# Splitting the rounding of context and tiles between ScalarE and VectorE, with reordered expert stage, in a decoder block

## The reference

```
x = x + attention(layernorm(x))           # 32 query heads, 8 key/value heads of 128, rope, causal
x = x + matmul(fake_quant(layernorm(x)), fake_quant(ctx))   # ctx 2 x 1024 x 1024
x = x + experts(layernorm(x))             # 64 experts of rank 8, the top 16 of 64 by a router, softmax gate
fake_quant(x): q = clip(round(x / s + z), 0, 255); return (q - z) * s
```

## Time and profile before

| what | value |
|---|---|
| time, median of 3 runs | 1343.87 us (1343.54 to 1347.83) |
| the profiled execution's own time | 1344.35 us |
| its span, first to last instruction | 1342.6 us |
| mean granted TensorE clock | 0.987 of full |
| TensorE busy | 1273.5 us, 95% |
| VectorE, ScalarE, GpSimd busy | 831.3, 772.8, 613.9 us |

### The profile page before, as it was taken

One profiled execution on the slowest core, in us unless ns is written; L12 is line 12 of the kernel. 1 busy time (PEld: TensorE's weight loads), 2 busy tenths in 40 slices (PEclk: granted clock), 3 DMA queues, 4 the chain that ended last, 5 costly groups with the idle time before them and its releaser, 6 DMA issues. The chain is left out here.

```text
span 1342.6 us, 19909 instructions
## 1 busy us (share of the span) xinstructions
PE 1273.5 (95%) x7016; PEld 1095.6 (82%) x7025; DVE 831.3 (62%) x1805; ACT 772.8 (58%) x1587; POOL 613.9 (46%) x454
## 2 busy tenths in 40 slices
PE   5899999999999999999999979899999998988998
PEld 4779998888888888888888868778888887667777
DVE  7797135555556555565555555456877769787753
ACT  3512237667777777777777768753333454654530
POOL 5677666678758677777776745310000000201100
PEclk9999999999999999999999989899999999989999
DMA  7033144548659468485673976888653485000001
GB/s 266 9 134 126 48 153 162 156 130 217 210 159 251 143 179 243 122 215 139 160 207 111 236 214 199 234 239 260 218 157 126 162 279 166 23 1 16 32 32 47
DMA packets 117122, 207.42 MB, mean 154 GB/s; under 512 B 10128, under 2 KB 51088, under 8 KB 113440
## 3 DMA queue, kind: packets, MB, share of 16 engines
q1 hardware_dynamic: 112992, 176.79, 39.9%
q0 software_dynamic: 4032, 29.36, 11.8%
HBM read 147.40 MB, written 88.08 MB: 175 GB/s over the span
## 5 line engine op out<-in xcount | busy, mean ns | idle before, releaser
L1225 DVE TENSOR_TENSOR pT_lo<-banks,pT_hi 128x512 fp32r<-128x512 f32 (+1 forms) x192 | 103.7, 596 | 184.9 <-ACT pT_hi L963 184.9
L1609 PE MATMUL banks<-ob_hi,oa_hi 128*128 128x512 f32 x384 | 149.7, 390 | 4.5 <-DVE ob_lo L1257 3.8
L1609 PE MATMUL banks<-ob_hi,oa_lo 128*128 128x512 f32 x384 | 149.4, 389 | 0.0
L1609 PE MATMUL banks<-ob_lo,oa_hi 128*128 128x512 f32 x384 | 149.4, 389 | 0.0
L1804 POOL TENSOR_TENSOR resid<-resid,colterm 128x1024 f32<-128x1024 f32 x8 | 19.8, 2490 | 274.4 <-ACT colterm L1861 184.4
L1567 PE MATMUL banks<-xc,nring_hi_a 128*128 128x512 f32 x448 | 140.0, 394 | 1.3 <-DVE q_made L1175 1.3
L1567 PE MATMUL banks<-xc,nring_hi_b 128*128 128x512 f32 x448 | 139.8, 393 | 0.0
L947 ACT CAST oa_hi<-oraw 128x1024 fp32r<-128x1024 f32 x48 | 50.4, 1050 | 146.9 <-PE banks L1609 142.7
L963 ACT CAST pT_hi<-banks 128x512 fp32r<-128x512 f32 (+1 forms) x192 | 86.5, 525 | 76.6 <-PE banks L1537 76.4
L1234 DVE CUSTOM_DVE_ANT_0 prob<-banks,mask 128x512 f32<-128x512 f32 (+3 forms) x256 | 109.8, 485 | 0.3 <-DVE resid L1153 0.3
L728 POOL TENSOR_TENSOR q_lo<-q_raw,q_hi 128x512 fp32r<-128x512 f32 x64 | 87.0, 1360 | 40.5 <-ACT q_hi L901 40.4
(11 more groups left out here) (245 smaller groups left out, 3483.2 us busy)
## 6 DMA issues: line engine op xcount, KB each, us to landing
q_raw<-qk_dram SPq DMA_DIRECT2D x64, 256.0 KB, 3.9
o_S<-o_st SPq DMA_DIRECT2D x64, 256.0 KB, 3.9
w<-in_L_attn_Wo SPq DMA_DIRECT2D x32, 512.0 KB, 6.5
oraw<-o_S SPq DMA_DIRECT2D x32, 512.0 KB, 3.7
nraw<-in_L_attn_Wq SPq DMA_DIRECT2D x28, 512.0 KB, 5.7
o_S<-o_S POOLq DMA_DIRECT2D x12, 1024.0 KB, 10.7
o_S<-o_N POOLq DMA_DIRECT2D x12, 1024.0 KB, 9.7
resid<-in_x SPq DMA_DIRECT2D x16, 512.0 KB, 6.4
```

What stands on the lines that cost most here:

```text
L1225: nc.vector.tensor_tensor(pT[1][:, sl], turned_chunk(turned, mixed, c), as32(pT[0][:, sl]), ALU.subtract).then_inc(pT_lo, 1)
L1609: ins = nc.tensor.matmul(step_bank(m, t), oa[a][:, s % 2, k, t * P:(t + 1) * P], ob[c][:, s % 2, k, :], start=(q == 0 and k == 0 and i == ...
```

## The change

It does the following. (a) At the start GpSimd makes w_low(3) ahead of the weight sums, and the sums wait until VectorE has normalised its four tiles. (b) `load_first(0)` and `load_first(1)` move ahead of the stores of turned heads, with weaker waits. (c) The copy of banks 6 and 7 after step 7 moves from ScalarE to VectorE. (d) The ctx rounding is split: ScalarE scales and clamps at 0 (Relu), VectorE takes the minimum with 255 and adds MAGIC, ScalarE takes off the constant (unmagic) into bf16. (e) The additions of p1 after product P5 are spread over four steps. (f) Tiles of x are rounded in the same three parts. (g) In the expert loop the transposes of the next tile (`x` fills) move ahead of turn_quantised and expand, and the parts of each tile are put in another order on ScalarE and VectorE.

In the order's rows, raw is the buffer of a tile being rounded, q its quantised bf16 form, norm and xe the normalised tile and its transposed parts, part the read-out product, zT the gated transposed values.

The diff, shortened (declarations, arguments and lines that only follow the same move are left out):

```diff
@@ -541,7 +542,8 @@
             if f == 0:
                 for n in (26, 27):
                     sp.wait_ge(o_kept[n % 2], o_count(n))
-                sp.wait_ge(job_read, 6 * NARROW)
+            if f < 2:
+                sp.wait_ge(job_read, 6 * NARROW - 1 + f)
             if f >= 2:
                 sp.wait_ge(fa_lo, f - 1)
             q, half = f % PAIRS, f // PAIRS
@@ -613,6 +615,8 @@
+            if u == LAST_JOB_UNIT + 1:
+                load_first(0)
...
+            if u == LAST_JOB_UNIT + 1:
+                load_first(1)
-                load_first(f)
+                if f >= 2:
+                    load_first(f)
...
@@ -797,10 +805,11 @@
         w_low(0)
         w_low(1)
         w_low(2)
+        w_low(3)
+        pool.wait_ge(ln_out_v, TPB)
         weight_sum(0, "S1")
         weight_sum(0, "S3")
         weight_sum(0, "S2")
-        w_low(3)
         for n in range(2 * TPB):
             turn_sum(n)
         w_low(4)
...
@@ -924,18 +933,19 @@
+            if f == 1:
+                act.wait_ge(q_kept[0], 64 * NARROW)
-        def keep_first(f):
-            if f % PAIRS == PAIRS - 1:
-                act.wait_ge(first_done, f + 1)
-                for n in range(2):
-                    nc.scalar.copy(p1[:, 2 * (f // PAIRS) + n, :], banks[:, 6 + n, :]).then_inc(first_read, 1)
+        def keep_second_pass():
+            act.wait_ge(first_done, FIRST_STEPS)
+            for n in range(2):
+                nc.scalar.copy(p1[:, 2 + n, :], banks[:, 6 + n, :]).then_inc(first_read, 1)
...
 
         def scale_ctx(n):
             act.wait_ge(ctx_in[n % 2], 16 * (n // 2 + 1))
-            nc.scalar.activation(raw[:, n % 2, :], raw[:, n % 2, :], ACT.Identity, bias=Z2, scale=R2
+            nc.scalar.activation(raw[:, n % 2, :], raw[:, n % 2, :], ACT.Relu, bias=Z2, scale=R2
                                  ).then_inc(c_scaled, 1)
+
+        def quant_ctx(n):
+            act.wait_ge(c_rounded, n + 1)
+            if n == 0:
+                act.wait_ge(one_made, 1)
+            nc.scalar.activation(q2[:, n, :], raw[:, n % 2, :], ACT.Identity, bias=unmagic[:, 0:1], scale=1.0
+                                 ).then_inc(c_quant, 1)
 
         root(0)
         ln_scale(1)
...
@@ -1060,17 +1073,20 @@
-        keep_first(FIRST_STEPS - 1)
+        keep_second_pass()
+            if 1 <= n:
+                quant_ctx(n - 1)
+        quant_ctx(2 * KT - 1)
-            nc.scalar.activation(raw[:, t, :], resid[:, t, :], ACT.Identity, bias=scl[:, 1, t:t + 1],
+            nc.scalar.activation(raw[:, t, :], resid[:, t, :], ACT.Relu, bias=scl[:, 1, t:t + 1],
...
             nc.vector.tensor_tensor(ob[1][:, f % 2, :, :], w00[:, 2 * q:2 * q + 2, :], as32(ob[0][:, f % 2, :, :]),
                                     ALU.subtract).then_inc(fb_lo, 1)
 
+        def keep_first_pass():
+            dve.wait_ge(first_done, PAIRS)
+            for n in range(2):
+                nc.vector.tensor_copy(p1[:, n, :], banks[:, 6 + n, :]).then_inc(first_read, 1)
+
...
@@ -1311,17 +1330,17 @@
-                elif p == "P5":
-                    link(nc.vector.tensor_tensor(rows(1, 1, tp), p1_pair(tp), rows(1, 1, tp), ALU.add))
-                    link(nc.vector.tensor_tensor(rows(1, 0, tp), p1_pair(tp), rows(1, 0, tp), ALU.add))
-
-        def quant_ctx(n):
+
+        def add_copy(tp, half):
+            dve.wait_ge(out_read, 2 * OUT.index("P7") + 2)
+            for t in (2 * tp, 2 * tp + 1):
+                dve.wait_ge(x_in[TPB + t], 32)
+            link(nc.vector.tensor_tensor(rows(1, half, tp), p1_pair(tp), rows(1, half, tp), ALU.add))
+
+        def round_ctx(n):
-            nc.vector.tensor_scalar(raw[:, n % 2, :], raw[:, n % 2, :], MAGIC, MAGIC, ALU.add, ALU.max
+            nc.vector.tensor_scalar(raw[:, n % 2, :], raw[:, n % 2, :], 255.0, MAGIC, ALU.min, ALU.add
-            dve.wait_ge(c_rounded, n + 1)
-            nc.vector.tensor_scalar(q2[:, n, :], raw[:, n % 2, :], MAGIC + 255.0, MAGIC + MIDDLE,
-                                    ALU.min, ALU.subtract).then_inc(c_quant, 1)
...
@@ -1413,6 +1432,8 @@
+            if (u, 1) in STEP_AT and STEP_AT[u, 1] == PAIRS - 1:
+                keep_first_pass()
@@ -1423,11 +1444,13 @@
-                quant_ctx(s - 4 * PAIRS)
+                round_ctx(s - 4 * PAIRS)
+            if m == 4 and 3 <= q < 7:
+                add_copy((q - 3) // 2, (q - 3) % 2)
...
@@ -1760,6 +1784,8 @@
+        if i + 1 < TT:
+            lb_order += [("x", 2 * i + 2), ("x", 2 * i + 3)]
...
@@ -1814,8 +1840,16 @@
-            nc.scalar.activation(v1[:, t % 2, :], resid[:, t, :], ACT.Identity, bias=scl[:, 1, t:t + 1],
+            nc.scalar.activation(v1[:, t % 2, :], resid[:, t, :], ACT.Relu, bias=scl[:, 1, t:t + 1],
+
+        def quantise(t):
+
+            act.wait_ge(v_rounded, t + 1)
+            if t >= 2:
+                act.wait_ge(q_turned, t - 1)
+            nc.scalar.activation(q1[:, t % 2, :], v1[:, t % 2, :], ACT.Identity, bias=unmagic[:, 0:1], scale=1.0
+                                 ).then_inc(v_quant, 1)
...
@@ -1900,23 +1938,26 @@
         root(2)
         copy_turned(3)
         exponentials(0)
-        late_root(TPB)
+        highs("x", (2, 3))
+        normalise(2)
         for i in range(1, TT):
-            highs("x", (2 * i, 2 * i + 1))
-            if i + 1 < TT:
-                normalise(i + 1)
-            if i + 3 < TT:
-                scale_tile(i + 3)
             if i + AHEAD < TT:
                 read_product(i + AHEAD)
             high("z", i - 1)
+            if i == 1:
+                highs("b", range(6, 8))
+            if i + 3 < TT:
+                late_root(i + 3)
+                scale_tile(i + 3)
             if i + AHEAD < TT:
                 root(i + AHEAD)
-            if i == 1:
-                highs("b", range(6, 8))
+            if i + 3 < TT:
+                quantise(i + 3)
             exponentials(i)
-            if i + 4 < TT:
-                late_root(i + 4)
+            if i + 1 < TT:
+                highs("x", (2 * i + 2, 2 * i + 3))
+            if i + 2 < TT:
+                normalise(i + 2)
             if i + 3 < TT:
                 copy_turned(i + 3)
         high("z", TT - 1)
...
@@ -1938,15 +1979,12 @@
-        def quantise(t):
+        def round_tile(t):
-            link(nc.vector.tensor_scalar(v1[:, t % 2, :], v1[:, t % 2, :], MAGIC, MAGIC, ALU.add, ALU.max))
-            if t >= 2:
-                dve.wait_ge(q_turned, t - 1)
-            nc.vector.tensor_scalar(q1[:, t % 2, :], v1[:, t % 2, :], MAGIC + 255.0, MAGIC + MIDDLE,
-                                    ALU.min, ALU.subtract).then_inc(v_quant, 1)
+            nc.vector.tensor_scalar(v1[:, t % 2, :], v1[:, t % 2, :], 255.0, MAGIC, ALU.min, ALU.add
+                                    ).then_inc(v_rounded, 1)
...
@@ -2033,31 +2074,37 @@
+        product_stats(1)
-        quantise(3)
+        round_tile(3)
+        product_stats(2)
+        lows("x", (2, 3))
-            lows("x", (2 * i, 2 * i + 1))
+            if i + AHEAD < TT:
+                row_term(i + AHEAD)
+                add_product(i + AHEAD)
+            low("z", i - 1)
+            if i == 1:
+                lows("b", range(6, 8))
+            if i + AHEAD < TT:
+                product_stats(i + AHEAD)
-                row_term(i + AHEAD)
-                add_product(i + AHEAD)
+                scale_of(i + AHEAD)
-                quantise(i + 3)
-            low("z", i - 1)
-            if i + AHEAD < TT:
-                scale_of(i + AHEAD)
-            if i == 1:
-                lows("b", range(6, 8))
+                round_tile(i + 3)
+            if i + 1 < TT:
+                lows("x", (2 * i + 2, 2 * i + 3))
...
@@ -2200,6 +2247,8 @@
+            if i + 1 < TT:
+                turn_fills("x", (2 * i + 2, 2 * i + 3))

```

More of the change, by code:

```diff
@@ L127, in build @@
         one = sb("one", [P, P], BF16)
+        unmagic = sb("unmagic", [P, 1], F32)
         banks = whole.enter_context(nc.psum_tensor("banks", [P, 8, 512], F32))
@@ L190, in build @@
             b_rows = sb4("b_rows", [P, D // P, NR], F32)
-            shared = (resid, ident, identb, stats, moments, rstd, lnw, mean_rstd, scal, calc, scl, one, raw,
+            shared = (resid, ident, identb, stats, moments, rstd, lnw, mean_rstd, scal, calc, scl, one, unmagic, raw,
                       a_rows, b_rows, q2, banks, KT, TT, TPB, H)
@@ L251, in attention @@
               A_w, B_w, proj, heads, narrow, outp, resid, ident, identb, stats, moments, rstd, lnw, mean_rstd, scal,
-              calc, scl, one, raw, a_rows, b_rows, q2, banks, KT, TT, TPB, H):
+              calc, scl, one, unmagic, raw, a_rows, b_rows, q2, banks, KT, TT, TPB, H):
     _, sem = held
@@ L677, in _ @@
         nc.gpsimd.tensor_copy(identb[:], ident[:]).then_inc(ident_made, 1)
+        nc.gpsimd.memset(unmagic[:], -(MAGIC + MIDDLE)).then_inc(one_made, 1)
         nc.gpsimd.memset(one[:], 1.0).then_inc(one_made, 1)
@@ L1036, in _ @@
```

(27 more changed lines are left out.)

## The result

The changed kernel takes 1356.98 us (median of 6 runs, 1352.64 to 1360.64) against 1344.62 (6 runs, 1343.54 to 1347.83) for the kernel before: ratio 1.0075, 95% interval 1.0058 to 1.0092, so 0.75% slower. (Every ratio here is the recorded estimate from all runs; the two medians divided give 1.0092, and elsewhere too they differ from the ratio by up to 0.0017.) Predicted was 1351.0, in the range 1339.5 to 1358. The profiled execution took 1352.64, the shortest of the six; its span is 1350.9 at a mean clock of 0.982.

What follows compares the result with a forecast made beforehand. TensorE, busy 95% of the time, was taken as the bound, other engines costing only where it waits. Terms −2.0, −6.5, −4.4, +2.3 and +17.6 sum to +7.0 on 1344.35, 1351.4, put at 1351.0 for the median; range 1339.5 to 1358.

Steps and rivals of the forecast that it cites:

- Start: At the start, VectorE's row-scale multiplications no longer held beside GpSimd's sums, so the fill begins earlier: −2.0 us.
- First step: First step of the output projection: earlier load of oraw removes a 4.6 us wait and the low clock behind it, −6.5.
- Step 8: Output projection, step 8: moving the copy to VectorE removes TensorE's 3.8 us wait and the half clock behind it, −4.4.
- fourth rival: First 900 us: waits move on to VectorE and half of 12.9 is lost, about 1357 us; chance 0.05.
- ctx: Ctx stage: loads no longer overlap, cycle 6.1 against 5.44 us, lag +6.1, less a 3.8 wait; net +2.3.
- third rival: Ctx stage: the reload of ctx is slower than its median, +7 instead of +2.3, 1355.7 us; chance 0.1.
- Expert loop: Expert stage: GpSimd's addition holds scale_of, TensorE waits 4.7, a tile costs +3.4; with the clock the stage costs +17.6.
- second rival: Expert loop: VectorE's scale_of gets past GpSimd's addition, TensorE idles 2.3, about 1339 us, faster; chance 0.2.
- the first four turns go this way: Expert loop, i = 1 to 4: each turn costs +3.4 over an old 19.06 us, 13.6 in all.
- stand behind other work of TensorE for the most part; I count 0 to 3 and take 0: Prologue of the expert stage: ScalarE's new instructions delay first products 0, 2 and 3; 0 to 3 us, taken as 0.
- The clock: Expert stage: idles of 4.7 us lower TensorE's clock, 1.7 × 3 = 5.1, and 1.1 at the first turn.
- first rival: Expert stage: idles of 4.7 don't lower the clock, stage costs 11.4, total 1344.7 us, no change; chance 0.2.

Runs made afterwards that it cites:

- e1_front: The change in attention() alone, with the expert stage of the kernel before; ratio 0.9952 to the kernel before.
- e2_expert: The change in mix_and_experts() alone, with attention() of the kernel before; ratio 1.0129 to the kernel before.
- e7_front_swap: e1_front with ScalarE taking off the constant of ctx tile n - 1 ahead of scaling tile n; 1334.35 us, ratio 0.9904 to the kernel before.
- e3_pool_late: The changed kernel with GpSimd's addition to tiles 4 to 7 waiting for VectorE's rounding instead of ScalarE's scaling; ratio 0.9992 to the kernel before.
- e6_warm_full: The changed kernel with 76 further TensorE transposes (120 for tile 4) ahead of turn_quantised of tiles 4 to 7; ratio 1.0041 to the kernel before.
- e4_warm: The changed kernel with 40 further TensorE transposes ahead of each turn_quantised of tiles 4 to 7; ratio 1.0067 to the kernel before.
- e9_stats_later: e7_front_swap with VectorE's product statistics moved behind the tile's rounding and zT_lo in the expert stage; ratio 0.9901 to the kernel before.

## Why the prediction was right, and where only its sum was

The forecast of 1351.0 is 6.0 short of the measured median and inside the range. The front was forecast at −10.6 and is −6.5 in e1_front's time; the expert stage was forecast at +17.6 and is +17.4 in e2_expert's, for reasons that were only partly the forecast ones. Term by term:

- **Start, −2.0.** Measured 3.6 alone (2.2 to 5.1). The wait of 4.21 fell to 1.00 and one of 2.83 on xc came, as the prediction's "t3 gives the rest back" has it; the two traces are 1.7 apart at 57 us and 1.3 at 790, which explains less than half of the 3.6.
- **First step, −6.5.** Right: 6.2 alone (3.6 to 8.6). In the trace of the changed kernel it shows as 5.6, since the half clock behind the wait before it (3.3 long in both traces, ending at 789.39 and at 790.65) lasted 1.0 longer there.
- **Step 8, −4.4.** The mechanism as put ("stood behind high parts that waited for a transfer") is right, but "ahead of nothing that waits for a transfer" is not enough: VectorE's copy stands behind low parts that wait for the same transfer. The wait went in the five traces in which the load landed early and stayed in the four in which it landed late. The copy took VectorE 1.28 for the 1.3 taken. The fourth rival (half of the 12.9 of the first 900 us lost) is borne out by e1_front: its trace is 6.2 ahead at the end of the first pass. There step 8 waits 0.18, but TensorE waits 2.83 at 809.13 for ob_lo, since ScalarE had stood idle 3.39 for another load of oraw; the changed kernel's trace has no such wait.
- **ctx, +2.3.** The cycle was right to 0.1 (6.0 for 6.1), and e7_front_swap shows its cause. The lag's price was too high: 4.2 by the traces of e1 and e7 for 6.1. The 13 cycles took 77.8 for 70.7, a lag of 7.1 and not 8.2, of which some 2.9 were hidden, not 2.1. (The sum's 0.63 a cycle should be 6.1 − 5.44 = 0.66, and the expert stage's 3.4 a tile is 22.4 − 19.06 = 3.3; neither matters.) The stage came out at +0.4 in the profiled execution; over all traces it takes 266.9 on average with the old rounding (five), 266.7 with the split (seven) and 262.4 with the split turned round (two). So the change as made costs nothing here, the lag's 4 being paid by the terms counted at −3.8. The third rival is out: the loads landed after 3.6 for 3.7 before.
- **Expert loop.** GpSimd's hold on scale_of, the point on which the second rival (1339, faster) hung, is what e3_pool_late removes. In turns 2 to 4 the wait was 4.05 for 4.7, the turn 23.3 to 23.9 for 24.1 with the clock, sum +13.8 for +15.3.
- **The step that failed** is "the first four turns go this way", with its other half, "stand behind other work of TensorE for the most part; I count 0 to 3 and take 0". Turn 1 cost 0.1, not 4.5: its wait of 7.05 replaced old waits of 2.85, 2.79 and 1.54, and the prediction took 19.06 for an old turn that in turn 1 had been 27.6. The prologue cost 7.0, not 0, 4 of it by the split: TensorE waited there for the copy queued behind ScalarE's quantising, and for low parts that came later. The two errors, −4.4 and +7.0, went into one sum, +17.6, that was measured as +18.1. That agreement is luck in these terms, not evidence for them.
- **The clock.** The first rival is out: e6_warm_full keeps the clock by filling the idle alone, and its four turns are 6.4 shorter in the trace, for the 6.2 that the forecast had for the clock. The bound "under 2.9 leaves the clock at 1.00" is out too: waits of 1.83 and 2.02 were followed by 0.79 in some turns and 1.00 in others; waits of 1.42 by 1.00 in every turn looked at.

## What to carry to other kernels

When one stage of a shared queue splits an operation into A on one engine and B on another, ask for each use what is queued behind B while it waits for A: here it cost nothing in the loop of the old order, 4 to 8 us ahead of it, and 4 to 6 in the ctx stage, where turning two instructions round gave them back. A VectorE instruction with two inputs from SBUF that starts beside a GpSimd addition waits for its end, even on one column (2.17 us here for 0.17), so move the GpSimd work to a place where VectorE has only single-input work: in e3_pool_late the instructions beside it kept their 0.15 to 0.23 us. And set marks at the same instructions in both traces before you believe a total: terms that cancel look like a correct forecast.

## What was not expected of the hardware

- A wait of TensorE of about 2 us is followed by the half clock sometimes. Behind the six waits of 1.83 to 2.04 of turns 2 to 4 in e3_pool_late and e4_warm, the granted clock over 8 us was 1.00 four times and 0.79 twice.
- One load of 256 KB landed after 5.7 to 7.0 us in seven traces and after 11.4 to 13.3 in seven, with nothing between.
- GpSimd's addition starting first, VectorE's instruction with two inputs from SBUF is held until it ends: with one column (2.17 us) both end together, with 512 columns (2.33 us, in e9_stats_later) VectorE ends 0.54 us later.
